# Four graph layers on one core: in layer 2 every second group of edges goes by chunks of 128 edges, with indirect row transfers

## The reference

```python
e_in = jnp.concatenate([x[src], x[dst]], axis=-1)
edge_new = relu(e_in @ We1 + be1) @ We2 + be2          # per edge
agg = jax.ops.segment_sum(edge_new, dst, num_segments=6250)
mesh_new = relu(concatenate([x, agg]) @ Wn1 + bn1) @ Wn2 + bn2
return x + mesh_new
```

## Time and profile before

| what | us |
|---|---|
| median of three runs | 6396.56 |
| profiled execution, its own time | 6402.61 |
| its span | 6400.8 |
| PE busy in the span | 5654.8 (88%) |
| DVE busy | 4415.6 (69%) |
| POOL busy | 1361.4 (21%) |
| layer 2's edges, 3636 to 5363 | 1727 |

### The profile page before, as it was taken

The page is one execution under the profiler, slowest core; times in us unless marked ns, Lnnn a source line. Parts: engine busy times, 40 slices in busy tenths (PEclk is TensorE's granted clock), DMA queues, the critical chain, the costliest instruction groups (busy, mean ns, idle before and its releaser), DMA issues. The chain is left out here.

```text
span 6400.8 us, 164226 instructions
## 1 busy us (share of the span) xinstructions
PE 5654.8 (88%) x58310; PEld 4935.2 (77%) x58310; DVE 4415.6 (69%) x7547; ACT 2021.1 (32%) x4615; POOL 1361.4 (21%) x1304
## 2 busy tenths in 40 slices
PE   3999987999999999999977799989999898789987
PEld 2888876888888888888865599989899897456656
DVE  7999933777777777777764566656666564378874
ACT  0000033333333333343433222222222221366641
POOL 1444455333333333333324200000000000300000
PEclk9999999999999999999989899999999998899976
DMA  7444312222222222222211232323333221100000
GB/s 119 154 152 152 146 54 87 85 82 82 85 85 81 84 88 84 83 84 85 84 39 39 75 106 104 111 101 106 105 107 107 101 105 50 47 17 0 0 1 22
DMA packets 206497, 528.37 MB, mean 83 GB/s; under 512 B 33555, under 2 KB 85398, under 8 KB 199318
## 3 DMA queue, kind: packets, MB, share of 16 engines
q1 hardware_dynamic: 195936, 518.35, 23.8%
q10 hardware_dynamic: 10179, 4.02, 0.3%
HBM read 485.12 MB, written 37.19 MB: 82 GB/s over the span
## 5 line engine op out<-in xcount | busy, mean ns | idle before, releaser
L1275 PE MATMUL ps<-kv_table,stage 128*128 128x256 bf16 x7644 | 1262.6, 274 | 65.3 <-DVE stage L1131 27.3
L1247 POOL TENSOR_TENSOR message<-message 128x512 f32<-128x512 f32 (+1 forms) x676 | 725.1, 1073 | 1511.8 <-ACT message L1209 1511.8
L1663 PE MATMUL ps<-a_table,stage 128*128 128x128 bf16 x7644 | 865.7, 223 | 87.7 <-issue 56.4
L1666 PE MATMUL ps<-window,stage 128*128 128x128 bf16 x7800 | 883.5, 223 | 0.0
L1290 PE MATMUL ps<-message,slot_hot 128*128 128x136 f32 x5200 | 782.4, 293 | 112.2 <-POOL message L1247 92.9
L1565 DVE TENSOR_TENSOR slot_hot<-iota,slots 128x512 f32<-128x512 f32 (+1 forms) x676 | 454.1, 672 | 614.6 <-PE ps L1678 604.8
L1278 PE MATMUL ps<-window,stage 128*128 128x128 bf16 x7800 | 866.7, 220 | 0.0
L1290 PEld LDWEIGHTS ps<-message,slot_hot 128*128 128x128 f32 x5200 | 653.0, 191 | 201.7 <-POOL message L1247 165.6
L1138 DVE TENSOR_TENSOR slot_hot<-iota,slots 128x512 f32<-128x512 f32 (+1 forms) x676 | 452.3, 669 | 499.0 <-PE ps L1290 499.0
L1678 PE MATMUL ps<-edge,slot_hot 128*128 128x130 f32 x4992 | 731.6, 290 | 70.3 <-issue 70.3
L1616 ACT ACTIVATE edge<-ps 128x512 f32<-128x512 f32 x624 | 374.0, 599 | 1303.6 <-PE ps L1678 1266.6
(11 more groups left out here) (335 smaller groups left out, 7619.2 us busy)
## 6 DMA issues: line engine op xcount, KB each, us to landing
stage<-lists SPq DMA_DIRECT2D x312, 768.0 KB, 4.1
edges<-in_edge_attr SPq DMA_DIRECT2D x52, 1984.0 KB, 7.7
stage<-lists SPq DMA_DIRECT2D x104, 896.0 KB, 5.5
window<-qkv_rows SPq DMA_DIRECT2D x52, 288.0 KB, 4.8
qkv_rows<-kv_table SPq DMA_DIRECT2D x26, 384.0 KB, 2.5
window<-ab_rows SPq DMA_DIRECT2D x52, 192.0 KB, 4.4
qkv_rows<-q_parts SPq DMA_DIRECT2D x26, 192.0 KB, 2.0
ab_rows<-a_table SPq DMA_DIRECT2D x26, 192.0 KB, 2.0
```

Source lines behind the costliest of these rows:

```text
L1247: pool.tensor_tensor(values, values, message[n % 2][:, 0:nt, D:D + HEADS].unsqueeze(3) .broadcast_to([P, nt, HEADS, HEAD]), ALU.mult).then ...
L1275: nc.tensor.matmul(kv_ps[n % 2][:, i, :], from_src, kv_table[:, tile, q, :], start=(q == 0), stop=(q == 2))
L1663: nc.tensor.matmul(edge_ps[n % 2][:, i, :], from_src, a_table[:, tile, q, :], start=(q == 0), stop=False)
L1666: last = nc.tensor.matmul(edge_ps[n % 2][:, i, :], own, window[d][:, (3 + q) * D:(4 + q) * D], start=False, stop=(q == 2))
```

## The change

In layer 2's edge stage the even groups (d = 0) go as before. The odd groups (d = 1) go in the edges' own order, in 31 chunks of 128 edges, by 8 steps of four chunks (the last has three):
- a[src] is fetched as whole f32 rows from DRAM by indirect transfers which POOL issues, one for 128 edges, 31 a pair (L1641 of the changed kernel), into 8 pieces of `x`'s space. For this `layer1_nodes` also stores a (`a_rows`) and x (`x_rows`), and x is loaded back at the end.
- PE gathers only b[dst], three matmuls a chunk (L1875), with one-hots made by DVE from a list of targets (`own_half`, L1722) that `prepare` stores (`target_rows`).
- DVE adds gather and rows (`sum_rows`, L1742); ACT's relu goes from SBUF to SBUF and has a second small copy for the SELF flag.
- Degrees: DVE adds the source one-hots of every unit to a bf16 table, `degree_sum`, in two halves (`count_tiles`, L1702), and sums the table once at the end. For odd groups the source lists are loaded for this alone, one at a time into `list_one` (`count_natural`, L1713).
- `edge`, `slot_hot` and the PSUM banks of the gather are threefold, and a pair has 21 steps, not 26.

Space is made by laying weights into one tile (`early`) and by sharing semaphores.

```diff
+    # prepare, ACT (after 26 PE transposes of rel and 7 copies)
+    act.dma_start(target_rows.rearrange("k (c p) -> c k p", p=P), targets_i[:, :, :]
+                  ).then_inc(targets_stored, 16)
+    act.wait_ge(targets_stored, 16)
...
     # layer1_nodes, DVE and SP, each tile
+    dve.wait_ge(rows_stored[l], STORED[1] + n * 64)
...
+    sp.dma_start(a_rows[columns(c), :].rearrange("(j p) f -> p j f", p=P),
+                 node_rows[l][:, :, 0:D]).then_inc(rows_stored[l], 16)
+    sp.wait_ge(x_kept, NTILES + c + 1)
+    sp.dma_start(x_rows[:, columns(c)], x[:, columns(c)]).then_inc(rows_stored[l], 16)
...
     # layer2_edges, SP, at the start
+    sp.dma_start(index_all[:, :, :], src_index[:, 0:NG * G].rearrange("p (k t g) -> p k t g", t=2, g=G)
+                 [:, :, 1, :]).then_inc(index2, 16)
+    sp.dma_start(targets[:, :, :], sort_rel.rearrange("p (k t) g -> p k t g", t=2)[:, :, 1, :]
+                 ).then_inc(natural_in2, 16)
+    sp.dma_start(same, sort_ids.rearrange("p (k t) w g -> p k t w g", t=2)[:, :, 1, 0, :]
+                 ).then_inc(natural_in2, 16)
...
+    # layer2_edges, POOL, each pair
+    for h in range(2):
+        pool.tensor_copy(index_now[h][:, 0:n], index_all[:, ds(i, 1), 16 * h:16 * h + n] ...)
+        for m in range(4 * h, 4 * h + 4):
+            pool.wait_ge(summed2, pair * 8 + m + 1)
+            for c in CHUNKS[m]:
+                pool.indirect_dma_start(a_nat[m][:, c - 4 * m, :], None, a_rows[:, :],
+                    bass.IndirectOffsetOnAxis(ap=index_now[h][:, c - 16 * h:c - 16 * h + 1], axis=0)
+                    ).then_inc(rows_in2[h], 16)
+    # after the last pair
+    pool.dma_start(x[:, :], x_rows).then_inc(x_back, 16)
...
+    # layer2_edges, DVE
+    def sum_rows(pair, n):
+        dve.wait_ge(gathered2, pair * NS + n + 1 + AHEAD)
+        dve.wait_ge(rows_in2[m // 4], (pair + 1) * 16 * HALVES[m // 4])
+        dve.wait_ge(scattered2, pair * NS + n + 1)
+        dve.tensor_tensor(edge_nat[n % 3][:, 0:nt, 0:D], edge_ps[n % 3][:, 0:nt, :], a_nat[m][:, 0:nt, :],
+                          ALU.add).then_inc(summed2, 1)
...
-                            if b in (1, 4, 7, 10):
-                                unit_degrees(pair, d, b // 3)
+                            if BATCHES <= n + 1 < NS:
+                                sum_rows(pair, n + 1)
+                            if n in (1, 4, 7, 10):
+                                count_unit(pair, n // 3)
+                            if n in (2, 5):
+                                own_half(pair, n // 3)
+                            if n == 10:
+                                count_natural(pair, 0)
+                            if n in (11, 12):
+                                count_natural(pair, n - 10)
+                            if n == BATCHES + 1:
+                                count_natural(pair, 3)
...
+    # layer2_edges, PE, gather of a step of chunks
+    for c in CHUNKS[m]:
+        for q in range(3):
+            last = nc.tensor.matmul(to[:, c - 4 * m, :], own_hots[m // 4][:, at:at + P],
+                                    window[1][:, q * D:(q + 1) * D], start=(q == 0), stop=(q == 2))
```

More of the change, by code:

```diff
@@ L954, in gnn_program @@
         qkv_done = sem("qkv_done")
-        qkv_stored = [sem(f"qkv_stored{l}") for l in range(LANES)]
         MB = HIDDEN // P
@@ L1333, in gnn_program @@
         ab_done = sem("ab_done")
-        ab_stored = [sem(f"ab_stored{l}") for l in range(LANES)]
         def nth1(n, q):
@@ L1456, in _ @@
                 def _(sp):
-                    for l in range(LANES):
-                        sp.sem_inc(ab_stored[l], 32)
                     with sp.Fori(0, STEPS) as n:
@@ L1475, in gnn_program @@
         window_in2 = [sem(f"window_in2_{d}") for d in range(2)]
+        list_in2 = sem("list_in2")
+        list_hot2 = sem("list_hot2")
+        natural_in2 = sem("natural_in2")
+        natural_set2 = sem("natural_set2")
+        index2 = sem("index2")
+        rows_in2 = [sem(f"rows_in2_{h}") for h in range(2)]
+        summed2 = sem("summed2")
         hots2 = sem("hots2")
@@ L1487, in gnn_program @@
         EXTRA = 2
+        CHUNKS = [range(4 * m, min(4 * m + 4, G)) for m in range(8)]
+        NS = BATCHES + len(CHUNKS)
+        AHEAD = NS + 1
+        HALF = 16 * P
+        HALVES = (16, G - 16)
+        assert NS % 3 == 0 and len(CHUNKS) == 8
         with ExitStack() as scope:
             stage = sb("stage2", [P, 8 * UT * P], BF16, scope=scope)
-            window = [sb(f"window2_{d}", [P, 6 * D], BF16, scope=scope) for d in range(2)]
-            slot_hot = [sb(f"slot_hot2_{i}", [P, 4, P], scope=scope) for i in range(2)]
@@ L1492, in gnn_program @@
[L1492 to L1495 removed]
+            window = [sb(f"window2_{d}", [P, (6 - 3 * d) * D], BF16, scope=scope) for d in range(2)]
+            slot_hot = [sb(f"slot_hot2_{i}", [P, 4, P], scope=scope) for i in range(3)]
@@ new lines, in gnn_program @@
+            degrees = sb("degrees", [P, NB], scope=scope)
+            targets = early[:, 0:PAIRS * G].rearrange("p (k g) -> p k g", g=G)
+            index_all = early[:, PAIRS * G:2 * PAIRS * G].bitcast(I32).rearrange("p (k g) -> p k g", g=G)
+            assert 2 * PAIRS * G <= 13 * D
+            index_now = [sb(f"index_now{h}", [P, 16], I32, scope=scope) for h in range(2)]
+            shift = sb("shift", [P, 2], scope=scope)
+            a_nat = [x[:, m * 4 * D:(m + 1) * 4 * D].rearrange("p (c f) -> p c f", f=D) for m in range(8)]
@@ L1561, in batch @@
-                    def batch(pair, g, n):
-                        b, s = n % BATCHES, pair * NB2 + n
-                        nt = len(batch_tiles(b))
+                        folded = hot[:, 0:(end - first_tile) * P].rearrange("p (t h s) -> p t h s", h=2, s=P // 2)
+                        for h in range(2):
+                            dve.wait_ge(degree2, 2 * done + h + 16)
+                            dve.tensor_tensor(degree_sum[:, first_tile:end, :], degree_sum[:, first_tile:end, :],
+                                              folded[:, :, h, :], ALU.add).then_inc(degree2, 1)
@@ new lines, in own_half, with batch @@
+                    def own_half(pair, h):
+                        n = min(HALF, SC - h * HALF)
+                        dve.wait_ge(list_in2, pair * 96 + h * 16 + 16)
+                        dve.wait_ge(gathered2, pair * NS + BATCHES + 4 * h + 4 - NS + AHEAD)
+                        dve.tensor_scalar(own_hots[h][:, 0:n], list_one[:, 0:n], shift[:, 1:2], None,
+                                          ALU.is_equal).then_inc(list_hot2, 1)
+                    def batch(pair, i, n):
+                        s, nt = pair * NS + n, batch_size(n)
+                        if n < BATCHES:
+                            number, numbers = slots[:, ds(i * 2, 1), 0, 4 * n:4 * n + nt], iota1[:, :]
+                        else:
+                            at = 4 * (n - BATCHES)
+                            number, numbers = targets[:, ds(i, 1), at:at + nt], iota
@@ L1677, in scatter @@
-                        for i, tile in enumerate(batch_tiles(b)):
-                            last = nc.tensor.matmul(ps[:, 6 + d, 0:D + EXTRA], slot_hot[n % 2][:, i, :],
-                                                    edge_of(d, b)[:, i, :], start=(tile == 0), stop=(tile == SELF))
+                        if n in (0, BATCHES):
+                            pe.wait_ge(added2, pair * 2 + d + 13)
+                        for i in range(nt):
+                            last = nc.tensor.matmul(ps[:, 6 + d, 0:D + EXTRA], slot_hot[n % 3][:, i, :],
+                                                    edge_of(n)[:, i, :], start=(n in (0, BATCHES) and i == 0),
+                                                    stop=(n in (BATCHES - 1, NS - 1) and i == nt - 1))
@@ L1688, in body @@
                     def body(pair, behind, ahead):
-                        for n in range(NB2):
-                            if n + 2 < NB2 or ahead:
-                                gather(pair + (n + 2) // NB2, (n + 2) % NB2)
+                        for n in range(NS):
+                            if n + 2 < NS or ahead:
+                                gather(pair + (n + 2) // NS, (n + 2) % NS)
                             if n == 2 and behind:
@@ L1720, in gnn_program @@
         y_scaled = sem("y_scaled")
-        y_stored = [sem(f"y_stored{l}") for l in range(LANES)]
         nth2 = 4 * NTILES
```

383 lines of the change are left out of this document (253 added, 130 removed).

## The result

The changed kernel takes 6767.85 us (median of four runs, 6758.43 to 6775.78) against 6398.99 us for the kernel before in the same comparison: a ratio of 1.0577, interval 1.0558 to 1.0597. It is 5.8% slower, where 6140 was forecast. The profiled execution has a span of 6772.8 us, 372.0 more than before.

The account below looks back on a forecast made before the run. PE was taken to bound layer 2's edge stage. From 6402.6 us, minus 421 (PE), plus 130 (DVE), plus 30 (outside the loop) gave 6141.6, then 6136, rounded 6140; own range 6050 to 6220 (chance 0.48), whole range 5990 to 6450.

Parts of the forecast that it names:

- What POOL gets: Layer 2's 31 indirect transfers a pair at 1.3 us each, 40 us plus 0.8, hidden under the pair.
- 1.75 and 2.08: POOL's us per transfer: up to 1.75 fetching costs nothing; from 2.08 POOL's bound makes the kernel slower.
- A: Layer 2's edges: POOL is the bound and the kernel gets slower, 6620 us at the upper bound; chance 0.19.
- PE's saving: Layer 2's odd groups: 31 chunks take 12.4 us where 50 tiles took 28.6; 16.2 us a pair, 421 in all.
- the turn: Layer 2's loop turn, PE idle 2.48 and 3.84 us for issue; with the rest, 9.1 us a pair left unchanged.
- DVE's tail: Layer 2, steps 10 to 20: DVE's 25.0 us chain delays PE, costing 5 us a pair, 130 us.
- the folds: DVE's 16 additions a pair into the degree table, 0.5 us each: 8.0 us, up to 15.
- the list's wait: DVE waits for degree lists through one buffer, about 1.9 and 1.3 us, 3.1 in all a pair.
- rival C: Layer 2: the turn and threefold buffers hide DVE's work, PE alone counts, 6012 us; chance 0.12.
- Rival B: Layer 2: DVE's 14 one-source tests a pair each wait 0.65 us for POOL's transfers; 6255 us, up to 6370; chance 0.18.
- Outside the loop: Starts, ends, `prepare`, `layer1_nodes` and the first and last pairs: 30 us added (15 to 60).
- the upper case: `prepare`'s target store, 806 pieces one after another, 27 us in place of 2; +8 taken (0 to 25).

Follow-up runs that it names:

- e16_best: Changed kernel with 204 semaphore increments at the start of PE's program, five rounds: 6014.26 us, ratio 0.940 to the kernel before.
- e1_no_rows: Changed kernel without its 806 indirect transfers and without VectorE's wait on them: 6012.47 us, ratio 0.9417.
- e3_pool_plain: Changed kernel with the 31 transfers a pair still issued by POOL, but plain, rows in order (wrong rows): 6017.21 us, ratio 0.9424.
- e7_before_pad52: Kernel before with 52 semaphore increments at the start of PE's program, nothing else: 6466.92 us, ratio 1.008.
- e8: Changed kernel, each indirect transfer also waiting for a PE gather, plus 204 semaphore increments at PE's program start: 6013.91 us, ratio 0.9383.
- e11: Changed kernel with 204 semaphore increments at the start of PE's program, first run of this version: 5999.87 us, ratio 0.9376.
- e10: Changed kernel with 32 semaphore increments in POOL's program ahead of its loop: 6051.15 us, ratio 0.9456.

## Why the prediction was wrong

**The step that failed** is in "What POOL gets": that a fetch "costs nothing while 31c + 0.8 stays under 55 us". The price was right: c = 0.95 + 0.30 = 1.25 us where 1.3 was taken, below both points that the prediction names, 1.75 and 2.08, and POOL waits 884 us. In its place the runs showed that PE lost 27 us a pair beside these transfers (78.4 against 50.8 to 51.2 in the kernels that differ by idle instructions), and 25 us more ahead of the first transposes (88.0 against 62.8 or 63.4). I looked for cover on POOL's clock only, and never asked whether what POOL does can stop another engine that shares no data with it. None of the rivals has that: A, the one of the slower side, names POOL as the bound and 6620 us, and is wrong in mechanism and time. I also argued from durations alone, and the place of the code appears nowhere.

**PE's saving** is right. By the three windows of 25 pairs above PE is busy 61.6 us a pair before and 45.9 in e16_best: 15.7 less, where 16.2 was forecast. A step of an odd group takes 4305.40 - 4303.78 = 1.62 us there (forecast 1.60):

```profile
4303.78 0.77 PEld L1877 LDWEIGHTS ps<-window,x 128*128 128x128 bf16 x12
4304.50 0.97 PEld L1889 LDWEIGHTS ps<-edge,slot_hot 128*128 128x128 f32 x8
4305.40 0.77 PEld L1877 LDWEIGHTS ps<-window,x 128*128 128x128 bf16 x12
```

PE's idle time is 5.1 us a pair before and 5.2 in e16_best, but it is not the same time: before it is mostly the turn, now it is the wait for DVE. So a pair loses 15.6 us (66.7 to 51.1), where the forecast, which kept the turn and added DVE's tail, had 66.4 to 55.

**The turn** did not stay. The forecast left its 9.1 us. In the first kernel instruction packets come through the whole of layer 2's pairs, in the changed one next to none. Packets within 3676 to 5314 before, and within 3800 to 5700 after:

```profile
q8 instruction: 217, 3.56, 0.9%
```

```profile
q8 instruction: 5, 0.08, 0.0%
```

With 12 matmuls a step in place of 24 in the odd groups' gathers, and 31 chunks in place of 50 tiles, PE's loop has 563 matmuls a pair in place of 808, and the packets say that it is no longer fetched anew each time. The wait for "issue" of the earlier trace rows, 70.3 us, has no counterpart: in e1_no_rows the only wait of PE itself in 24 pairs is the one for DVE (view of waits, 3762 to 4954, PE alone):

```profile
PE ps L1881 <- DVE slot_hot L1728: 106.0, 54, 3.6
```

The Trainium skill ("Runtime: NRT & Kernel Launch", Instruction fetch mechanics) gives PE 128 KiB of instruction memory, 2048 instructions, refilled in blocks of 16 KiB, and says that prefetch is purely sequential and that a taken branch whose target isn't in the current two pages forces a fetch. The block agrees with the packets here (3.56 MB / 217 = 16 KB). The rule of the two pages, 512 instructions, does not agree: 5 packets in 24 pairs say that a loop of some 1,200 instructions (an estimate, from 563 matmuls with a weight load each) goes back to its start without a fetch. I did not weigh that page in the prediction, and it bore on the turn.

**DVE's tail** is right in kind and size: PE waits 106.0 / 24 = 4.4 us a pair for slot_hot in e1_no_rows, forecast 5, and 5.2 us a pair is all that PE idles in e16_best; the folds take 0.56 us (0.5), and the list's wait in the changed kernel is 91.4 us over 61 times, 1.5 each (1.9 and 1.3 at two places a pair). So rival C, which had it hidden, is wrong, although its 6012 us is what the kernel takes at a good place: it is reached by a turn that vanished, not by a tail that did.

**Rival B** has its mechanism in part and its price wrong. The changed kernel's medians of 616 and 620 ns do not settle it, as POOL's transfers are spread over a longer pair there. The same test, the second of a unit, in e16_best and in e1_no_rows, which has no transfers (ns: least, median, most):

```profile
L1696 DVE TENSOR_SCALAR stage<-stage,lane x104: 600/754/824, 3660.3 to 4951.4; 128x1536 bf16<-128x1536 int16 x78, 128x1792 bf16<-128x1792 int16 x26
```

```profile
L1689 DVE TENSOR_SCALAR stage<-stage,lane x104: 600/615/683, 3701.1 to 4960.2; 128x1536 bf16<-128x1536 int16 x78, 128x1792 bf16<-128x1792 int16 x26
```

So beside indirect transfers it takes 0.14 us more in the median. In e3_pool_plain, with POOL's plain transfers, the median is 615 as well; the first test of a unit has 620 and 618 ns, with a longest of 798 and 682. All 312 one-source tests of the lists together take 207.2 us in the one and 196.9 in the other, 0.4 us a pair, where B had 14 tests that wait 0.65 us each.
The Trainium skill ("SBUF — State Buffer", Who interferes with whom) has a test in a two-port mode and POOL's descriptors wait for one another for the whole instruction. No run shows the mode; the trace agrees that the two meet, and the longest of these tests, 824 ns, is 0.14 us over the longest without transfers.

**Outside the loop** 30 us were forecast (15 to 60). Measured in e16_best: start of the stage +5.7 (12), its end +3.2, the way to layer 1's edges +7.1, layer 1's nodes +21.2 (forecast +3), layer 2's nodes and layer 3 -15.5 (0). The last two have no cause shown; in e7_before_pad52, too, which differs from the kernel before by PE's idle instructions alone, all that follows layer 2's pairs is 11 us shorter. The target store went as in the upper case: while it ran out, 103 to 113 us, the transfers' share was 0.08, about one of 16 engines. `prepare` ended 8.7 us later in the changed kernel, near the forecast's +8, and 3 to 10.5 us later in the others that have the store. The prediction's sentence that this case would add 12 us does not follow from its own terms: 27 us begun near 85 end at 112, 5 after the 107 at which `prepare` ended. What was not foreseen at all is +45.3 in layer 1's edges, whose text the change does not touch: the 26 transposes in `prepare` put 52 instructions ahead of it. e7 adds 40 us to the kernel before by 52 idle ones, and with 204 more e8, e11 and e16 are back at 2260 to 2274, so the place is the cause.

**The sum** with the sizes measured, from 6402.6: 25 distances from pair to pair at -15.6, -390; the stalls, 25 x 27.3 + 25 = +707; the last group, which now has neither 50 tiles nor a next pair's gathers in it, 8.5 us in place of 21.3, -13; layer 1's edges +45; all else outside the pairs about +22. That is 6774, and the profiled execution took 6774.6. It is an account of where the time lies, from the same traces, and no proof of the causes.

## What to carry to other kernels

A loop's cost has a part that no duration shows: whether its instructions are fetched again at each turn, and where they lie. When a stage whose text did not change gets longer or shorter, or an engine idles for "issue" inside a step whose inputs are there, count the instruction packets in the stretch and move the code by a few dozen idle instructions before theorising on the edit; one such run (e10 or e11) would have shown in the first set what four others hid. And an experiment that edits one engine's program moves its code: without a control that moves it and does nothing else, it shows nothing about the thing edited.

## What the runs showed of the hardware

- An indirect transfer of 128 rows of 512 B occupies POOL for 0.95 us, with 0.30 to the next; a plain one of the same size 0.53 to 0.58.
- PE's loop of 808 matmuls a pair is fetched at 8.8 packets of 16 KB a pair at one place and 3.9 at another (layer 1's edges: 2306.6 and 2266.9 us, e7_before_pad52 and the kernel before); one of 563 matmuls hardly at all (5 packets in 24 pairs).
- With PE's and POOL's code at unlucky places, PE and SP take 0.70 us for each instruction while POOL makes indirect transfers, and layer 2's pairs go from 51 to 78 or 79 us. DVE and ACT show no such delay. A shift by 32 instructions of one of the two codes ends it, one by 256 of PE's does not.
- Beside indirect transfers a one-source test of 128x1536 or 128x1792 int16 on DVE takes a median of 754 ns, 615 without them (the line's 104 tests, e16_best and e1_no_rows).
